# Expert layers on sorted tokens in slots of one expert, the decay attention with folded weight products, and all of it in one block

## What is computed

```python
x = x + L0_attn(L0_cond(x))        # 16 heads of 8, then 16 heads of 64 with rotary positions
x = x + L0_ffn(L0_cond2(x))        # a quaternion rotation, then experts
x = x + L1_attn(L1_cond(x))        # experts, then 8 heads of 128 with decay
x = x + L1_ffn(L1_cond2(x))        # 16 heads of 8, then a ternary network with a convolution

# L0_ffn: 8 experts, each token uses the best 2
h = relu(flat_x @ W1[e] + b1[e]); y = h @ W2[e] + b2[e]            # 128 -> 512 -> 128
final_output = final_output + y * w[:, None]                       # w is 0 for unpicked experts

# L1_cond: 8 experts, the best 2, three layers
h1 = relu(x @ W1[e] + b1[e]); h2 = relu(h1 @ W2[e] + b2[e]); out_e = h2 @ W3[e] + b3[e]   # 128 -> 256 -> 256 -> 128

# L1_attn
A = (q k^T * scale) * decay * lamw; y = A v; out = y @ Wo.T + x    # then a layernorm
```

## Time and profile before

| | us |
|---|---|
| median of 3 runs | 715.18 |
| lowest, highest | 711.69, 717.57 |
| profiled execution: span from first to last instruction | 711.2 |
| TensorE busy | 558.2 (78%) |
| VectorE busy | 461.7 (65%) |
| ScalarE busy | 295.9 (42%) |
| GpSimd busy | 186.7 (26%) |

### The profile page before, as it was taken

One profiled execution on the slowest core, in us unless ns is written; L12 is line 12 of the kernel. 1 busy time (PEld: TensorE's weight loads), 2 busy tenths in 40 slices (PEclk: granted clock), 3 DMA queues, 4 the chain that ended last, 5 costly groups with the idle time before them and its releaser, 6 DMA issues. The chain is left out here.

```text
span 711.2 us, 10053 instructions
## 1 busy us (share of the span) xinstructions
PE 558.2 (78%) x3794; PEld 397.6 (56%) x3794; DVE 461.7 (65%) x1036; ACT 295.9 (42%) x631; POOL 186.7 (26%) x147
## 2 busy tenths in 40 slices
PE   2374686569999978979879999999999678778542
PEld 2152575546665845736644767766676557656421
DVE  1369985955756487494851434667777978988663
ACT  0133354134444334444444343343555465646441
POOL 1546724610501161240301000130303043133210
PEclk9997988769999999999998999999999999999655
DMA  9200000000222211111213222112110000000000
GB/s 302 94 1 1 1 2 0 1 0 1 61 60 60 61 31 30 31 30 31 60 31 118 63 73 56 49 30 61 31 31 5 1 5 5 0 5 5 5 4 4
DMA packets 32895, 25.56 MB, mean 36 GB/s; under 512 B 6448, under 2 KB 29360, under 8 KB 32592
## 3 DMA queue, kind: packets, MB, share of 16 engines
q1 hardware_dynamic: 32368, 24.62, 11.7%
q10 hardware_dynamic: 480, 0.32, 0.2%
HBM read 24.40 MB, written 0.52 MB: 35 GB/s over the span
## 5 line engine op out<-in xcount | busy, mean ns | idle before, releaser
L450 ACT ACTIVATE hid<-PS,expert_b 128x512 f32<-128x512 f32 x128 | 87.5, 687 | 120.2 <-PE PS L418 86.9
L418 PE MATMUL PS<-featT,expert_w 128*128 128x512 f32 x192 | 98.9, 627 | 4.9 <-DVE xres L495 2.3
L434 PEld LDWEIGHTS PS<-expert_w,hid 128*128 128x128 f32 x768 | 88.7, 192 | 15.5 <-ACT hid L450 9.8
L434 PE MATMUL PS<-expert_w,hid 128*128 128x128 f32 x768 | 91.5, 276 | 0.9 <-ACT hid L450 0.9
L638 POOL TENSOR_TENSOR cond_kbd<-cond_qkv,const 128x2048 f32<-128x2048 f32 x16 | 59.9, 3741 | 63.4 <-ACT cond_qkv L723 63.3
L863 POOL TENSOR_TENSOR rot_sh<-rot_sh,const 128x1024 f32<-128x1024 f32 x16 | 52.4, 3295 | 38.4 <-DVE rot_sh L1036 38.4
L425 PE MATMUL PS<-hid,expert_w 128*128 128x512 f32 x128 | 60.8, 601 | 0.2
L418 PEld LDWEIGHTS PS<-featT,expert_w 128*128 128x128 f32 x192 | 32.0, 195 | 44.2 <-ACT hid L450 21.5
L495 DVE SCALAR_TENSOR_TENSOR xres<-PS,gatew,xres 128x128 f32<-128x128 f32 x64 | 18.0, 343 | 59.3 <-PE PS L434 59.3
L650 POOL TENSOR_SCALAR cond_st<-cond_st 128x1 f32<-128x1 f32 x16 | 5.8, 364 | 173.9 <-ACT cond_zn L738 173.7
L785 DVE STREAM_TRANSPOSE cond_ptbd<-cond_sm 32x512 f32<-32x512 f32 x64 | 45.0, 703 | 1.2
(11 more groups left out here) (221 smaller groups left out, 1092.7 us busy)
## 6 DMA issues: line engine op xcount, KB each, us to landing
expert_w<-in_moe_w_dram SPq DMA_DIRECT2D x48, 256.0 KB, 2.9
expert_w<-in_moe_w_dram SPq DMA_DIRECT2D x32, 128.0 KB, 2.5
wqk<-in_attn_qk_dram SPq DMA_DIRECT2D x2, 1024.0 KB, 6.2
wv<-in_attn_v_dram SPq DMA_DIRECT2D x2, 512.0 KB, 7.2
wout<-in_attn_out_dram SPq DMA_DIRECT2D x2, 512.0 KB, 8.4
last_b<-in_moe_last_b_dram SPq DMA_DIRECT2D x2, 512.0 KB, 6.1
xres<-in_x_dram SPq DMA_DIRECT2D x1, 512.0 KB, 5.2
cond_w<-in_cond_w_dram SPq DMA_DIRECT2D x2, 256.0 KB, 5.7
```

Source lines behind the costliest of these rows:

```text
L418: mm = nc.tensor.matmul(full(at), w[:, P * f:P * f + P], featT[:, BANK * half:BANK * half + BANK], start=True, stop=True)
L434: mm = nc.tensor.matmul(full(at, E * j, E * j + E), h[:, 2 * layer + c, P * j:P * j + P], w[:, lo:lo + E], start=(c == 0), stop=(c == nf - 1))
L450: nc.scalar.activation(hid[e % 2][:, c, :], full(at), ACT.Relu, bias=WBIAS[g % WB][:, c:c + 1]).then_inc(ring_read[number % 2], 1)
```

## The change

**One block.** After the preparation there is one block, and the order is by a written-out table, `TIMES`: each step has one number for each of its calls, and `run_in_time_order` sorts by them. A line of it is `"r_mask_scores": (47.7, 64.3, 82.4, 95.9, 125.4, 151.9, 186.7, 216.3)`.

**Sorted tokens.** For each of the four jobs (first half layer 0, first half layer 1, second half layer 0, second half layer 1, called job 0 to 3) the best two experts are picked for each token (`choose`), the picks of each expert are counted by products with a triangular matrix (`count`, bf16), and each pick gets a row in a list of 15 slots of 128 rows (`places`), where slots 0 to 7 belong to experts 0 to 7 and the others to whichever expert runs over (`EXTRA`, at most 7). `scatter` writes the tokens to `slots_x` in DRAM, by 8 indirect DMAs of 128 rows on GpSimd's queue; `gather` brings the results back from `slots_y` with 8 more, after all 15 stores, and `combine` adds the two rows of a token with their weights. The biases are one product with the weights (L680), where L502 was. For each slot SyncE issues the weights (for 8 to 14 with the number of the expert read from a register), the tokens and the store; TensorE transposes the slot, makes `hidden_a` and `hidden_b` (two outputs of 128x128 each) and `slots_out`. `relu_a` and both copies are ScalarE's. **The last 256 inner columns of the tile are relieved by VectorE**: `relu_b`. A slot has 9 products of 128x128, in both layers.

**Decay attention folded.** In the same block, before they are first used, `M = Wq Wk^T` and `W = Wv Wo` are made for each head (24 transpositions, products and copies). A tile then has `project` (8 products with M), `scores` (4, out 32x256), one weighting, `times_u` (4, with the input itself) and `output` (8 with W). Keys, values and their copies are gone.

**Rotation folded.** `rotate_right` and `rotate_left` are one product; the matrix is made in the preparation. `cond_kbd` and `rot_sh` have one buffer where they had more.

What stands where, engine by engine. **TensorE, where the first half's layer 1 was worked off between the second half's steps (before):**

The core of the diff:

```diff
-        def mixture_plan(half, jobs):
-            rows = [[("mean", 0, 0, 0)] if half == 0 else [], [("transpose", 1, 0, 0), ("route", 1, 0, 0)], [("transpose_u", 1, 0, 0), ("gates", 1, 0, 0)]]
-            first = [[("hidden", 0, e, f) for f in range(FF0 // P)] for e in range(EXPERTS)]
-            rows[0] += first[0]
-            for e in range(EXPERTS):
-                rows[0] += (first[e + 1] if e + 1 < EXPERTS else []) + [("out", 0, e, 0)]
-            inner = [[("hidden", 1, e, f) for f in range(FF1 // P)] for e in range(EXPERTS)]
-            rows[1] += inner[0]
-            for e in range(EXPERTS):
...
-                    pe.wait_ge(w_loaded[g % WB], loads_up_to(g))
-                    mm = nc.tensor.matmul(full(at), w[:, P * f:P * f + P], featT[:, BANK * half:BANK * half + BANK], start=True, stop=True)
-                elif kind == "hidden2":
-                    for c in range(FF1 // P):
-                        pe.wait_ge(*read_of(numbers["hidden", 1, e, c]))
-                    for c in range(FF1 // P):
-                        lo = FF1 + FF1 * c + P * f
-                        mm = nc.tensor.matmul(full(at), w[:, lo:lo + P], h[:, c, :], start=(c == 0), stop=(c == FF1 // P - 1))
...
+            def load_weights(i):
+                job, half, layer, s = job_of(i)
+                w, fields = W[i % WB], ((("w1", 1, FF0), ("w2", FF0 // P, E)), (("w1", 1, FF1), ("w2", FF1 // P, FF1), ("w3", FF1 // P, E)))[layer]
+                if i >= WB:
+                    sp.wait_ge(m_out_ps, i - WB + 1)
+                if s < EXPERTS:
+                    here = lambda name: d[f"moe{layer}_{name}"][s:s + 1]
...
+                sp.dma_start(slot_x[i % XB][:], xs[half][P * s:P * s + P, :]).then_inc(x_loaded[i % XB], 16)
+            def store_slots(i):
+                job, half, layer, s = job_of(i)
+                sp.wait_ge(m_y_ready, i + 1)
+                sp.dma_start(ys[half][P * s:P * s + P, :], slot_y[i % YB][:]).then_inc(m_stored[i % YB], 16)
+            return [("m_load_weights", load_weights), ("m_load_slots", load_slots), ("m_store_slots", store_slots)]
+        def mixture_pool(pool):
+            def scatter(i):
+                job, n = divmod(i, HT)
+                half, layer = job // 2, job % 2
+                if i == 0:
+                    pool.wait_ge(loaded["blank"], 16 * 2)
+                pool.wait_ge(place_ready, job + 1)
+                if layer == 0:
+                    pool.wait_ge(f_ready, HT * half + n + 1)
+                src = (featn, xres)[layer]
+                for j in range(2):
+                    nc.gpsimd.indirect_dma_start(xs[half], bass.IndirectOffsetOnAxis(place_u[job % 2][:, j, n:n + 1], 0),
+                                                 src[:, HT * half + n, :], None).then_inc(scattered[job % 2], 16)
...
+            def transpose_slots(i):
+                pe.wait_ge(x_loaded[i % XB], 16 * (i // XB + 1))
+                claim(pe, (MB_[i % 2],), (m_y_ready, i + 1))
+                nc.tensor.transpose(full(MB_[i % 2], 3 * P, 4 * P), slot_x[i % XB][:], k["ident"]).then_inc(m_xT_ps, 1)
+            def hidden_a(i):
+                job, half, layer, s = job_of(i)
+                pe.wait_ge(m_xT_ready, i + 1)
+                pe.wait_ge(w_loaded[i % WB], weights_up_to(i))
+                for f in range(2):
+                    mm = nc.tensor.matmul(full(MB_[i % 2], P * f, P * f + P), W[i % WB][:, P * f:P * f + P], slot_xT[i % 2][:], start=True, stop=True)
+                mm.then_inc(m_a_ps, 1)
+            def hidden_b(i):
+                job, half, layer, s = job_of(i)
+                other = MB_[(i + 1) % 2]
+                pe.wait_ge(m_xT_ready, i + 1)
+                pe.wait_ge(w_loaded[i % WB], weights_up_to(i))
+                claim(pe, (other,), (m_b_ready, i + 1))
+                if layer == 0:
+                    for f in range(2, 4):
+                        mm = nc.tensor.matmul(full(other, P * f, P * f + P), W[i % WB][:, P * f:P * f + P], slot_xT[i % 2][:], start=True, stop=True)
+                else:
+                    pe.wait_ge(m_a_ready, i + 1)
+                    for f in range(2):
+                        for c in range(2):
+                            lo = FF1 + FF1 * c + P * f
+                            mm = nc.tensor.matmul(full(other, P * (2 + f), P * (2 + f) + P), W[i % WB][:, lo:lo + P], hid[:, i % 2, c, :], start=(c == 0), stop=(c == 1))
+                mm.then_inc(m_b_ps, 1)
+            def slots_out(i):
+                job, half, layer, s = job_of(i)
+                pe.wait_ge(m_a_ready, i + 1)
+                pe.wait_ge(m_b_ready, i + 1)
+                first, lo = ((0, FF0), (2, 3 * FF1))[layer]
+                for c in range(first, 4):
+                    mm = nc.tensor.matmul(full(MB_[i % 2], 0, E), hid[:, i % 2, c, :], W[i % WB][:, lo + E * (c - first):lo + E * (c - first) + E], start=(c == first), stop=(c == 3))
+                mm.then_inc(m_out_ps, 1)
...
+            def relu_a(i):
+                act.wait_ge(m_a_ps, i + 1)
+                for c in range(2):
+                    ins = nc.scalar.activation(hid[:, i % 2, c, :], full(MB_[i % 2], P * c, P * c + P), ACT.Relu, bias=WBIAS[i % WB][:, c:c + 1])
+                ins.then_inc(m_a_ready, 1)
+            def copy_out(i):
+                act.wait_ge(m_out_ps, i + 1)
+                if i >= YB:
+                    act.wait_ge(m_stored[i % YB], 16 * (i // YB))
+                nc.scalar.activation(slot_y[i % YB][:], full(MB_[i % 2], 0, E), ACT.Copy).then_inc(m_y_ready, 1)
...
+            def relu_b(i):
+                dve.wait_ge(m_b_ps, i + 1)
+                for c in range(2, 4):
+                    ins = nc.vector.tensor_scalar(hid[:, i % 2, c, :], full(MB_[(i + 1) % 2], P * c, P * c + P), WBIAS[i % WB][:, c:c + 1], 0.0, ALU.add, ALU.max)
+                ins.then_inc(m_b_ready, 1)
...
+            def combine(i):
+                job, n = divmod(i, HT)
+                half, layer = job // 2, job % 2
+                dve.wait_ge(biasing, 4 * job + 4)
+                dve.wait_ge(m_gathered[n], 32 * (job + 1))
+                to = (xres, acc)[layer][:, HT * half + n, :]
+                nc.vector.scalar_tensor_tensor(out=to, in0=picked[:, 0, n, :], scalar=weight[job % 2][:, n, 0:1], in1=to, op0=ALU.mult, op1=ALU.add).then_inc(mix_step, 1)
+                dve.wait_ge(mix_step, own_mix.next())
+                nc.vector.scalar_tensor_tensor(out=to, in0=picked[:, 1, n, :], scalar=weight[job % 2][:, n, 1:2], in1=to, op0=ALU.mult, op1=ALU.add).then_inc(m_done, 1)
...
+            def project(n):
+                if n == 0:
+                    pe.wait_ge(folding, 8)
+                pe.wait_ge(gating, 8 * (n // HT) + 2)
+                claim(pe, (PB, PB + 1), (p_ready, n + 1))
+                for h in range(LH):
+                    mm = nc.tensor.matmul(full(PB + h // 4, P * (h % 4), P * (h % 4) + P), log_M[:, h, :], uT[:, P * n:P * n + P], start=True, stop=True)
+                mm.then_inc(p_ps, 1)
+            def scores(n):
+                pe.wait_ge(p_ready, n + 1)
+                claim(pe, (SB_,), (a_ready, n + 1))
+                for b in range(SEQ):
+                    mm = nc.tensor.matmul(full(SB_, 0, LH * S)[S * b:S * b + S, :], uT[:, P * n + S * b:P * n + S * b + S], pT[:, :, S * b:S * b + S], start=True, stop=True)
+                mm.then_inc(s_ps, 1)
+            def times_u(n):
+                pe.wait_ge(a_ready, n + 1)
+                claim(pe, tuple(range(YB_, YB_ + SEQ)), (yT_ready, n + 1))
+                for b in range(SEQ):
+                    mm = nc.tensor.matmul(full(YB_ + b, 0, LH * S), acc[S * b:S * b + S, n, :], aT[S * b:S * b + S].rearrange("p h t -> p (h t)"), start=True, stop=True)
```

1756 lines of the change are left out of this document (970 added, 786 removed), and 40 rows, old and new, of the table TIMES.

## The result

The changed kernel takes 756.77 us (median of 4 runs, 755.73 to 761.53) against 715.08 before: 1.062 times the time, interval 1.0561 to 1.0675. It is slower, and outside the range of 655 to 738. The profiled execution has a span of 753.9.

A forecast was written before the change was run, and what follows sets the result against it. It took tiles without experts to be bound by VectorE with handoffs, and TensorE to be full with experts. Terms from start to last store summed to 696.5, plus 4 outside the span: 700 us against 715.18, range 655 to 738.

The forecast's parts named there:

- nine stretches: Whole span cut as the forecast's sum was, from start to tail: 696.5 us in all.
- The ring: Slots of jobs 1 to 3: each engine waits for the next; a turn 5.7 us in job 1, 3.2 in job 2.
- job 2: First half's layer 1 step in the sum: 15 slots alone on TensorE at the high clock, 15 x 3.2 = 48 us.
- rival A: Slots of jobs 1 and 3: clock stays high, job 1 falls by 27 us and job 3 by some 15; 658; chance 0.20.
- B: GpSimd's queue: an indirect DMA costs 1.9 us instead of 1.0, 32 on the path, +29, so 729; chance 0.14.
- stage 1: Attention of 8 tiles in layer 0 with job 0 beside it: 260 us, ends 237 and 288.
- VectorE's 218 us at a fill of 0.84: Attention of layer 0 and job 0: VectorE's remaining work over the last three tiles' fill gives 260 us.
- Rival C: Attention of layer 0: fills as badly as at 80 to 120, 0.756, so 288 instead of 260, 728; chance 0.14.
- the way to job 3: From job 2's last store through gathers, combine, routing, sorting, scatters and load: 38 us with handoffs.
- Routing 6.7, sorting 3, eight scatters at 1.0: Between jobs 2 and 3: pieces in us, routing and sorting, then eight indirect writes, within the 38.
- the tail: Tiles 4 to 7 after job 3: first tile 55 us, other three 57 at 19 each, a store 1.5.
- 45 turns of the ring: Slots of jobs 1, 2 and 3, 15 each, claimed on the path: 86, 48 and 82 us.

The follow-up runs named there:

- experiment 2: Changed kernel with six more products of 128x128, needed by nobody, in each of job 1's 15 slots; 728.6 us, ratio 1.0195.
- experiment 1: Changed kernel with the relu of the last 256 inner columns on ScalarE instead of VectorE; 748.5 us, ratio 1.049.
- experiment 5: Changed kernel with job 0's 15 slots, gather and sums moved behind the attention of layer 0; 823.4 us, ratio 1.152.
- Experiment 7: Changed kernel with job 3's picking and its first slot's transposition and copy earlier in the rows; 753.7 us, ratio 1.055.
- Experiments 6: Changed kernel with the last four tiles' steps evenly spaced, each tile 19.5 later than the one before; 766.4 us, ratio 1.073.
- experiment 12: Kernel of experiment 4 with products that nobody needs in TensorE's gaps of the last three tiles' networks; 723.6 us, ratio 1.014.
- experiment 9: The changed kernel run again as it is; 748.6 us, ratio 1.047.
- experiment 4: Changed kernel with own PSUM banks for a slot's parts and another order of TensorE's steps in jobs 1 and 2; 716.4 us, ratio 1.0032.

## Why the prediction was wrong

The sign of it was wrong, and no single term accounts for that: seven of nine stretches came out longer, and the sum was short by 57.4 us of 753.9. The median lay 2.9 above the span instead of 4.

**Right** were the mechanisms of the slots. The ring was read correctly from the code and priced from the earlier trace rows: 5.7 us forecast for a turn of job 1, 5.81 measured; 3.2 for job 2 at the high clock, 3.19 measured over its last nine turns; job 3 82 against 78.8. The clock at 0.5 through job 1 came as forecast, and experiment 2 shows that it costs 23 to 25 us there (rival A said 27). Two of the prediction's numbers were slips: the products of a slot are 4.07 us at the low clock by the prediction's own terms, not 4.7, so 71% of a turn and not 82 (62.84 of 89.1 measured); and the terms of a turn at the high clock add up to 3.6, not 3.9. By 4.07 of 5.2 job 2 would have been at 78% and not at 90, so the high clock forecast for it had less behind it than was said; it came, after 12 us. VectorE and TensorE were to be busy below 400 us each, and were 438.9 and 494.4.

Rival A did not come about, nor B as priced: an indirect DMA follows the one before it after 1.27 us (the median; 1.25 to 1.58), not 1.0 and not 1.9. Three of job 1's eight writes:

```profile
310.20 0.97 POOL L625 DMA_INDIRECT slots_x<-xres,place_u  x1 [0.30 <-issue]
311.48 0.97 POOL L625 DMA_INDIRECT slots_x<-xres,place_u  x1 [0.30 <-issue]
312.75 0.97 POOL L625 DMA_INDIRECT slots_x<-xres,place_u  x1 [0.30 <-issue]
```

The fixed 2.0 us of the Trainium skill's "DMA: Bandwidth & Descriptors" (section "Anatomy of one DMA — SWDGE (gpsimd) path") is not the price of one in a row: the trace has 1.27 from one to the next, and by 2.0 the forecast would have been 732. In three of the stretches 32 of them stand on the path, some 0.28 more each, 9 us of the 57.

**The step that failed first is stage 1**, +15.7. "VectorE's 218 us at a fill of 0.84": the 218 were right (217.77 measured), and so was the fill as long as there was a next tile. The two stretches around the last tile of the attention:

```profile
250.00:271.80 21.80, 18.96 (x161) 16.73 (x160) 17.28 (x25) 10.75 (x32) 7.55 (x4) 1.00 0.42 116
271.80:297.70 25.90, 14.62 (x110) 12.18 (x109) 11.38 (x25) 7.38 (x19) 10.17 (x11) 0.70 0.24 67
```

Up to 271.8 VectorE works 206 of 250 us, 0.83; in the last 25.9 it works 11.4, since one tile's chain is left and nothing beside it. A sum of work over a fill leaves out this run-out. That is the arithmetic of the miss; VectorE's work is not its cause, since 7.6 us less of it (experiment 1) and no slots at all (experiment 5) ended the stage at the same place. What sets its end stays open. Rival C (288 at a fill of 0.756) is 12 above the 275.7 where the forecast is 16 below, and experiment 5 refutes its reason: it is not the slots' relus.

**The second, and the largest, is the way to job 3**, +16.9. "Routing 6.7, sorting 3, eight scatters at 1.0": the time of the earlier trace rows was taken for a chain that runs alone, but it stands in the rows of engines that do decay attention.

| piece | forecast | measured |
|---|---|---|
| gates, last store, to the first gather | 5 + 2.5 | 6.5 |
| gathers and sums | 12.8 | 14.2 |
| routing and sorting | 9.7 | 17.0 |
| writes, to the slot's load | 9.5 | 11.6 |
| load, to the first transposition | 2 + 1.5 | 10.4 |

Routing and sorting, and the first slot's start, make 14 of the 17. On VectorE the picking stood behind one group of L1506 of 6.85 us, which takes 2.84 elsewhere. Of its six operations the one that met GpSimd's L979 took 3.71 us and the next one, beside L986, 1.18; the others took 0.45:

```profile
490.16 6.85 DVE L1506 COPY_PREDICATED arena<-levelmask,z 128x256 f32<-128x256 int32 x6
...
490.91 3.61 POOL L979 TENSOR_TENSOR cond_kbd<-cond_qkv,const 128x2048 f32<-128x2048 f32 x1
...
645.21 2.84 DVE L1506 COPY_PREDICATED arena<-levelmask,z 128x256 f32<-128x256 int32 x6
```

On TensorE the first slot, whose tokens were asked for at 516.21, stood behind L1459, L1018 and L1584:

```profile
516.21 1.75 SPq L605 DMA_DIRECT2D slot_x<-slots_x  x4
...
521.68 3.75 PE L1459 MATMUL PS<-log_W,arena 128*128 128x128 f32 x16 [0.58 <-ACT arena L1495]
...
526.61 0.42 PE L685 MATMUL PS<-const,slot_x 128*128 128x128 f32 x1
```

Experiment 7 confirms the second of these and not the first: with the slot moved up, 10.4 became 3.5; with the picking moved up, the wait for GpSimd fell on another operation.

The third is the tail, +10.7: 17.6 us for each of the last three tiles where 19 were forecast, but 78 from the last sum to the first output where 64 were. All four decay attentions end before the first output. Experiments 6 and 12 did not shorten the tail by more than 1.4 us; what bounds it is not shown. The fourth is job 2, +8.8, of which some 4 are the one long wait on ScalarE and its after-effect (experiment 9), and the rest its first three turns at the low clock, 3.8 to 4.7 us each where 3.2 were put.

**Why it is slower at all** is another question, and there the prediction's sentence that 45 turns of the ring are on the path was right and well priced: jobs 1 to 3 were forecast at 216 us and took 225. The other stretches, the run-out in stage 1 and the way to job 3 above all, are 49 of the 57. What the change did is this: beside the attention it put job 0's slots in the place of dense products and took job 1 away, and the attention ended 74 us earlier; then it put job 1, with its writes, and the way from job 2 to job 3 behind it, alone. Experiment 5 measures the same from the other side: 15 slots beside the attention 0 us, alone about 70. Of the slower result, experiment 4 shows where 32 to 40 us lie: the ring's order and banks in jobs 1 and 2, the clock's share included. With them put right the sorted kernel ties with the dense one; no variant here beats it.

## What to carry to other kernels

Before counting the work that a change removes, ask for each piece whether it will stand beside other work or alone: 15 slots cost nothing beside the attention and 70 us alone. A chain of small steps over several engines should be put into the rows so that each engine has a piece of the next turn to do while it waits, with buffers of its own for each part: this gave 42 us of 146 here, where the relu on the other engine gave none. When stages are sized by an engine's work over its fill, add the run-out of the last item. And a chain priced from a stretch where it ran alone gets longer in the rows of busy engines: 9.7 us of routing and sorting became 17.0.

## What the runs showed of the hardware

- The granted clock answers to work of any kind: with six idle products a slot it was 0.95 where it had been 0.50, and the stretch took 64.4 us instead of 89.1 with more in it (experiment 2). In the last two networks the same raised it from 0.50 to 1.00 and gave 1.6 us of 15.8 each (experiment 12).
- Indirect DMAs of 128 rows of 512 bytes from GpSimd's queue follow each other after 1.27 us (median; 1.25 to 1.58), 32 writes and 32 reads alike (0.96 busy, 0.30 between).
- Six COPY_PREDICATED of 128x256 on VectorE took 2.84 us, and 6.62 and 6.85 beside GpSimd multiplications of 3.61 and 1.25; the one that met the first took 3.49 and 3.71 instead of 0.45. An addition of two 128x32 tiles took 3.29 instead of 0.19 in the same way (experiment 7).
- The changed kernel gave 756.8 and 748.6 on two occasions, while the kernel before gave 715.1 and 714.7 on the same two.
